# One bank for the first feed-forward product, two pairs of banks in turn for the scores, and new orders for all engines

## The reference, cut to what matters

```
A  x = x + relu(x @ Wd_b.T + bd) @ Wu_b.T + bu         # Wd_b, Wu_b: weights of this batch
   x = layernorm(x) * w + bias, + row of the batch
   h = layernorm(x) * g1 + b1 ;  q, k, v = h @ W_qkv.T
B  s = q @ k.T / 4  (16 heads of 16) ;  p = softmax(s) ;  o = p @ v
C  x = x + (o @ W_o.T) * a1
   h = layernorm(x) * g2 + b2
   x = x + (gelu_tanh(h @ W_f1.T) @ W_f2.T) * a2        # 256 -> 1024 -> 256
D  h = rmsnorm(x) * scale ;  u = h @ up_w.T             # 256 -> 2048
   h = gelu(u[gate]) * u[value] ;  h = quantised to int8 steps per row
   out = x + h @ ternary(down_w).T                      # 1024 -> 256
```

## Time and profile before

| | |
|---|---|
| median of 3 runs | 933.14 us (932.55 to 935.09) |
| the profiled execution's own time | 935.74 us |
| its span, first to last instruction | 933.9 us |
| PE busy | 843.1 us (90%) |
| DVE, ACT, POOL busy | 565.4, 510.9, 231.2 us |
| granted TensorE clock, mean | 0.946 |

### The profile page before, as it was taken

One profiled execution on the slowest core, in us unless ns is written; L12 is line 12 of the kernel. 1 busy time (PEld: TensorE's weight loads), 2 busy tenths in 40 slices (PEclk: granted clock), 3 DMA queues, 4 the chain that ended last, 5 costly groups with the idle time before them and its releaser, 6 DMA issues.

```text
span 933.9 us, 15916 instructions
## 1 busy us (share of the span) xinstructions
PE 843.1 (90%) x5852; PEld 633.5 (68%) x5852; DVE 565.4 (61%) x1063; ACT 510.9 (55%) x796; POOL 231.2 (25%) x333
## 2 busy tenths in 40 slices
...
GB/s 344 365 366 252 248 138 124 148 80 122 62 203 38 135 97 114 120 78 156 47 187 47 188 47 188 46 173 61 154 76 142 65 127 80 104 80 25 24 12 12
DMA packets 58477, 118.48 MB, mean 127 GB/s; under 512 B 6336, under 2 KB 15936, under 8 KB 55696
## 3 DMA queue, kind: packets, MB, share of 16 engines
...
...
## 4 chain that ended last, share of the span: by engine, by line
PE 74%; issue 9%; DMA 7%; DVE 4%; ACT 2%; SPq 2%; POOL 2%; POOLq 0%; DVEq 0%; ACTq 0%
PE bank L486 30%; PE bank L692 11%; PE pair_s L653 6%; PE pair_s L618 5%; PE pair_t L639 5%; PE pair_t L486 4%; DMA hyp<-in_hyper 3%; PE bank L737 3%; PE bank L664 3%; PE bank L567 2%; PE bank L729 1%; PE bank L561 1%; DVE oq L1145 1%; DMA wc<-in_cols 1%; PE bank L574 1%
## 5 line engine op out<-in xcount | busy, mean ns | idle before, releaser
L851 ACT ACTIVATE Pr<-pair_t 128x1024 f32<-128x1024 f32 x128 | 131.3, 1026 | 125.2 <-PE pair_t L639 121.5
L1121 DVE TENSOR_REDUCE nmax<-pair_s 128x4 f32<-128x1024 f32 x128 | 155.8, 1217 | 34.5 <-PE pair_s L618 33.9
L692 PE MATMUL bank<-wf,G 128*128 128x256 f32 x512 | 123.0, 387 | 0.1
L486 PE MATMUL bank<-wup_hi,hD_hi 128*128 128x512 f32 x256 | 109.4, 427 | 4.8 <-POOL hD_lo L1316 4.1
L1344 POOL TENSOR_TENSOR x<-x,xcr 128x512 f32<-128x512 f32 x16 | 20.5, 1281 | 358.1 <-DVE x L1179 358.1
L692 PEld LDWEIGHTS bank<-wf,G 128*128 128x128 f32 x512 | 93.3, 190 | 15.5 <-issue 0.2
L486 PE MATMUL bank<-wup_lo,hD_hi 128*128 128x512 f32 x256 | 102.0, 398 | 0.0
L486 PE MATMUL bank<-wup_hi,hD_lo 128*128 128x512 f32 x256 | 101.9, 398 | 0.0
L618 PE MATMUL pair_s<-Kp,Qp 64*128 64x256 f32 x512 | 66.1, 337 | 21.7 <-DVE nmax L1121 13.0
L895 ACT ACTIVATE gl<-bank,rsD 128x512 f32<-128x512 f32 x64 | 44.1, 689 | 63.6 <-PE bank L486 63.4
L1189 DVE SCALAR_TENSOR_TENSOR hd<-bank,rsD,gl 128x512 f32<-128x512 f32 x64 | 47.9, 748 | 46.2 <-PE bank L486 34.7
...
## 6 DMA issues: line engine op xcount, KB each, us to landing
...
Qp<-qk_scratch SPq DMA_DIRECT2D x64, 256.0 KB, 3.7
Kp<-qk_scratch SPq DMA_DIRECT2D x64, 256.0 KB, 3.6
...
cur_scratch<-gen SPq DMA_DIRECT2D x16, 256.0 KB, 10.1
xT_t<-in_xT SPq DMA_DIRECT2D x16, 256.0 KB, 4.2
```

What stands on the lines that cost most here:

```text
L486: mm = pe.matmul(dst, l, r, start=first and i == 0, stop=last and i == 2)
L692: mm = pe.matmul(bank[5][:, r * D:(r + 1) * D], G[:, k, r * P:(r + 1) * P], wf2[:, k, :], start=k == 0, stop=k == FT - 1)
L851: act.activation(Pr[:, p % 4, :, :].rearrange("p a n -> p (a n)"), pair_t[:, :, :].rearrange("p a n -> p (a n)"), ACT.Exp, scale=DH ** -0. ...
L1121: dve.tensor_reduce(nmax[:, n % 2, :, p % GP, :], pair_s[:, :, :].rearrange("p a (r n) -> p a r n", r=RT), AX.X, ALU.max, negate=True).the ...
```

## The change

- `B.s` slice `p` writes `pair[p % 2]`, and so does `B.t` slice `p`. A slice waits for the reader of the slice two before it. `s0` and `s1` wait for the exponentials of `t6` and `t7` of the batch before, `t0` for the maximum of `s6`, and `t1` for the copy of `m1`.
- `B.m1` moves to bank 2 (`m0` stays in bank 0); `B.o` moves to bank 5.
- All four `C.f` are in bank 5, so `f1` to `f3` each wait for both GELUs of the one before. `C.g0` waits for `tr0`, `B.o0` for the last GELU, `B.o2` for `gate2`, DVE's read of the second feed-forward result.
- `A.k` moves to bank 4 and waits until DVE has read `A.q`; `A.v` waits until DVE has read `A.k`.
- SP waits for all loads of the last turn's heads before it stores new queries or keys.
- The orders of all engines are new, those of head and tail too.

```diff
 FULL = {
     "SP": """
-        C.tc A.load B.m0 B.m1 A.qs A.ks A.ql0 A.ql1 A.kl0 A.ql2 A.kl1 A.kl2 D.y0 A.ql3 D.y1 A.kl3""",
+        C.tc B.m0 A.load B.m1 A.qs A.ql0 A.ql1 A.ks A.ql2 D.y0 A.ql3 A.kl0 A.kl1 A.kl2 A.kl3 D.y1""",
     "PE": """
-        B.s0 A.down C.proj B.s1 A.up D.u0 B.s2 D.u1 C.ht B.s3 D.u2 C.f0 B.m0 C.f1 C.f2 B.s4 A.ht C.f3 B.s5 D.u3 B.t0 B.s6 A.q D.qt0 B.s7 B.t1 A.k D.y0
-        B.t2 B.m1 B.o0 B.t3 C.g0 B.t4 B.o1 A.v B.t5 D.qt1 C.g1 C.g2 B.t6 C.g3 B.t7 D.y1 B.o2 B.o3 C.xt""",
+        B.s0 C.proj D.u0 B.s1 A.down B.s2 B.s3 A.up C.ht D.u1 B.m0 C.f0 D.u2 B.s4 B.s5 C.f1 A.ht D.u3 C.f2 B.s6 B.s7 A.q D.qt0 C.f3 B.m1 B.t0 B.t1
+        D.y0 A.k B.t2 B.t3 B.o0 B.t4 B.o1 B.t5 B.t6 D.qt1 C.g0 C.g1 C.g2 C.g3 B.t7 D.y1 B.o2 B.o3 C.xt A.v""",
     "ACT": """
-        A.down D.u0 C.lnb D.u1 C.ht D.u2 C.f0 A.lnb C.f1 C.f2 A.ht C.f3 D.u3 B.t0 D.qt0 A.q B.t1 A.k B.t2 B.t3 B.t4 B.t5 B.t6 D.qt1 B.t7 A.v C.xt""",
+        D.u0 A.down C.lnb C.ht D.u1 D.u2 C.f0 A.lnb C.f1 A.ht D.u3 C.f2 A.q D.qt0 C.f3 B.t0 B.t1 B.t2 B.t3 B.t4 A.k D.qt1 B.t5 B.t6 B.t7 C.xt A.v""",
     "DVE": """
-        B.s0 C.proj B.s1 C.ln A.up D.u0 B.s2 A.lna D.u1 A.lng B.s3 A.ln B.p0 B.m0 D.quant0 B.s4 D.u2 A.cur B.s5 D.u3 B.s6 B.s7 B.p1 A.q B.m1 A.k
-        D.quant1 D.y0 B.o1 C.g3 D.y1 B.o3""",
+        B.s0 C.proj C.ln B.s1 D.u0 B.s2 B.s3 B.p0 A.up A.lna B.m0 D.u1 A.lng A.ln D.quant0 D.u2 B.s4 B.s5 D.u3 B.s6 B.s7 B.p1 B.m1 A.q D.quant1 A.cur
+        B.o1 A.k D.y0 C.g3 D.y1 B.o3""",
     "POOL": """
-        A.down C.proj C.ln A.up C.ht A.lna A.ln A.ht C.g3 C.xt""",
+        A.down C.proj C.ln C.ht A.up A.lna A.ln A.ht C.g3 C.xt""",
 }
...
 HEAD, turn 0:
-    SP   A.load A.qs A.ks A.ql0 A.kl0 A.ql1 A.ql2 A.ql3 A.kl1 A.kl2 W.late A.kl3
+    SP   W.late A.qs A.load A.ks A.ql0 A.kl0 A.ql1 A.ql2 A.kl1 A.ql3 A.kl2 A.kl3
-    ACT  W.qkv A.down A.lnb A.ht A.q W.fa A.k A.v
+    ACT  A.down W.qkv A.lnb A.ht W.fa A.q A.k A.v
 TAIL, turn 17, PE:
-    C.proj D.u0 D.u1 C.ht D.u2 C.f0 C.f1 C.f2 C.f3 D.u3 C.g0 D.qt0 C.g1 D.y0 C.g2 C.g3 D.qt1 D.y1 C.xt
+    C.proj D.u0 D.u1 C.ht D.u2 C.f0 D.u3 C.f1 D.qt0 C.f2 D.y0 C.f3 D.qt1 C.g0 C.g1 C.g2 C.g3 D.y1 C.xt
...
+        pair = [pair_s, pair_t]
-        F_BANK = [bank[5], bank[2], bank[3], bank[5]]
...
                 def a_k():
-                    if with_c:
-                        pe.wait_ge(act_c, at(ACT_C, "gelu7", c))
-                    else:
-                        past(pe, dve_a, DVE_A, "klo1", a, 1)
+                    pe.wait_ge(dve_a, at(DVE_A, "qlo1", a))
...
                 def a_v():
-                    pe.wait_ge(dve_a, at(DVE_A, "qlo1", a))
+                    pe.wait_ge(dve_a, at(DVE_A, "klo1", a))
...
                 def b_s(p):
-                    if p == 0:
-                        past(pe, dve_m, DVE_M, f"t{NG - 1}", b, 1)
-                        past(pe, dve_o, DVE_O, "tr1", b, 1)
-                    elif p % GP == 0:
-                        pe.wait_ge(dve_m, at(DVE_M, f"t{p // GP - 1}", b))
+                    if p < 2:
+                        past(pe, act_t, ACT_T, f"exp{NP - 2 + p}", b, 1)
                     else:
-                        pe.wait_ge(dve_s, at(DVE_S, f"max{p - 1}", b))
+                        pe.wait_ge(dve_s, at(DVE_S, f"max{p - 2}", b))
+                    if p == GP:
+                        pe.wait_ge(dve_m, at(DVE_M, "t0", b))
...
                 def b_t(p):
-                    if p:
-                        pe.wait_ge(act_t, at(ACT_T, f"exp{p - 1}", b))
-                    elif with_c:
-                        pe.wait_ge(act_c, at(ACT_C, "gelu5", c))
+                    if p >= 2:
+                        pe.wait_ge(act_t, at(ACT_T, f"exp{p - 2}", b))
+                    elif p == 1:
+                        pe.wait_ge(dve_m, at(DVE_M, "t1", b))
                     else:
-                        past(pe, act_t, ACT_T, f"exp{NP - 1}", b, 1)
+                        pe.wait_ge(dve_s, at(DVE_S, f"max{NP - 2}", b))
...
                 def b_o(g):
                     if g == 0:
                         pe.wait_ge(act_a, at(ACT_A, "v", b))
-                        pe.wait_ge(dve_s, at(DVE_S, f"max{NP - 1}", b))
+                        if with_c:
+                            pe.wait_ge(act_c, at(ACT_C, "gelu7", c))
                     if g == 2:
                         pe.wait_ge(dve_o, at(DVE_O, "tr0", b))
+                        if with_c:
+                            pe.wait_ge(dve_c, at(DVE_C, "gate2", c))
...
                 def c_f(n):
                     if n == 0:
                         pe.wait_ge(pool_c, at(POOL_C, "lo", c))
-                    if n == 3:
-                        pe.wait_ge(act_c, at(ACT_C, "gelu1", c))
+                    else:
+                        pe.wait_ge(act_c, at(ACT_C, f"gelu{2 * n - 1}", c))
...
                 def c_g(n):
-                        if not isinstance(a, int) or a < NB:
-                            pe.wait_ge(dve_a, at(DVE_A, "klo1", a))
+                        if b < NB:
+                            pe.wait_ge(dve_o, at(DVE_O, "tr0", b))
...
 SP, at ("A", "qs") and at ("A", "ks"):
+                        if a >= 1:
+                            for j in range(4):
+                                sp.wait_ge(heads_in[j], 32 * a)
```

More of the change, by code:

```diff
@@ L72 @@
     "SP": """
[L73 to L76, removed]
+        0: W.late A.qs A.load A.ks A.ql0 A.kl0 A.ql1 A.ql2 A.kl1 A.ql3 A.kl2 A.kl3 1: B.m0 A.load A.qs B.m1 A.ql0 A.ks A.ql1 A.ql2 A.kl0 2: C.tc 1:
@@ L79 @@
[L79 to L82, removed]
```

103 lines of the change are left out of this document (54 added, 49 removed).

## The result

| | before | after |
|---|---|---|
| median of 4 runs of each on one chip | 934.12 us | 951.79 us (950.68 to 954.84) |
| the profiled execution, and its span | 935.74, 933.9 us | 954.84, 953.0 us |
| granted TensorE clock, mean | 0.946 | 0.935 |

The ratio is 1.0191, with a 95% interval of 1.0176 to 1.0206: 1.9% slower. The prediction said slower, at 938 us, with a range of 914 to 950. The direction was right and the size wrong, by 14 us. The profile of after is the slowest of its four executions, so the profiles differ by 19.1 us of span and the medians by 17.7.

The account below looks back on a forecast made before the run. PE, busy 90% of the span, was taken as the bound. Nine `FULL` turns +3.6 us, tail +3.2 and head -2 sum to +4.8, on the median 933.14 giving 938 us; range 914 to 950.

Parts of the forecast that it names:

- Edges, -2.0 us a turn: `FULL` turn on PE: nine fewer edges between score slices and full-array matmuls, 0.19 us each (1.7), plus 0.3 at `s0`.
- Waits, +2.4 us a turn: `FULL` turn on PE: added waits before `f1` 1.0, `f0` 0.5, around `t3` 0.6, and small ones at `o1`, `s3`, `C.ht`.
- wait 1: `FULL` turn: `C.f1` waits for both GELUs of `f0`, behind `D.u2` and a table load on ACT: 1.0 us.
- Tail, +3.2 us: Turns 14 to 17: +1.2, +0.7, +0.4 and +0.9 us, from fewer edges saved, added waits and turn 17's shared bank.
- Head, -2 us: First turns: removed waits set against later work of turn 2; -2 us taken, from -14 to +6.
- all 13.0 us of waits for maxima: Head: PE's waits of score slices for the previous slice's maximum, ten places, all 13.0 us expected to go.
- 1.48 us of the weights' high part: Head: the weights' high part ahead of `dn`, 1.48 us expected to go.
- projection and feed-forward of turn 2 come some 5 us later: Head: `o3` of turn 1 now stands behind `s0` of turn 2, which waits for its keys: some 5 us.
- Covered by `qt0`, `f3`, `m1`, `t0`, `t1`, `y0` (about 4 us; uncovered it would be some 2 us): `A.q` and `A.k` in one bank: `k`'s wait for DVE's reading of `q` hidden by other PE work.
- rival C: Keys come late, so `s0` of each turn waits: 956 us at two more us a turn, 947 at one; chance 0.12.

Follow-up runs that it names:

- unjoin: Changed kernel with `D.qt1` placed between `t5` and `t6` on PE in `FULL` turns, one slice pair less and two edges more: 956.5 us, a turn of 49.53 us.
- tail_full: Changed kernel with turns 14 and 15 written out in `FULL`'s order on every engine, banks untouched: 950.2 us, ratio 1.0145 to the kernel before.
- tail17: Changed kernel with turn 17's four feed-forward products in banks 5, 2, 3, 5, in the old order except `qt1` ahead of `g3`: 951.5 us, ratio 1.0160.
- head_m1: Changed kernel with turn 1's `B.m1` and `B.t1` ahead of `A.q`, `A.k` behind `t3`, DVE's order to match: 952.6 us, ratio 1.0195.
- fix_bank: head_fix plus head_bank, that is, the reordered head with turn 0's `A.k` in bank 5: 939.0 us, ratio 1.0046 to the kernel before.
- head_fix: Changed kernel with turns 0 and 1 reordered, stage A's chain first, and the up weights' low part moved to turn 2; banks kept: 946.5 us, ratio 1.0126.
- best2: best plus head_bank, and turns 14 and 15 in `FULL`'s order with `C.f0`'s GELUs ahead of `D.u2`: 926.3 us, ratio 0.9898 to the kernel before.
- best: head_fix plus tail17, with ACT taking `C.f0`'s GELUs ahead of `D.u2` in `FULL` and turns 14 to 16: 935.6 us, ratio 0.9996 to the kernel before.
- head_bank: Changed kernel with turn 0's `A.k` in bank 5, waiting for nothing, and `A.v` waiting only for `A.q`'s reading: 955.3 us, ratio 1.0210.
- spload_bank: spload and head_bank together on the changed kernel: 949.6 us, ratio 1.0173 to the kernel before.
- spload: Changed kernel with only SyncE's turn 0 list altered: load of turn 1's sequence first, late weights at the end: 952.1 us, ratio 1.0196.
- head_o3: Changed kernel with `B.o3` of turn 1 ahead of `B.s0` of turn 2 on PE and DVE: 952.4 us, ratio 1.0173.
- head_early: Changed kernel with SyncE's load first in turn 0 and turn 1's `A.down`, `A.up` ahead of its score slices, DVE's order to match: 950.6 us, ratio 1.0149.
- chain1: head_m1 and head_o3 together, with the up weights' low part (4.4 us on DVE) moved from turn 1 to turn 2: 951.9 us, ratio 1.0178.

## Why the prediction was wrong

**Edges, -2.0 us a turn: right.** unjoin measured 0.18 us an edge against 0.19, so nine are 1.6. The measured turn less what its waits cost by starts is 49.18 - 2.2 = 47.0 us, where the prediction had 47.1. The edges at the values' products were taken at 0.19 without a row, and no run isolates them; nor does a row say whether `m1` next to `o0`, both 128*32, is an edge, so the count is nine or eight.

**Waits, +2.4 us a turn: right in kind and place, 2.2.** By starts 0.94 for `f1` (predicted 1.0), 0.5 for `f0` (0.5), 0.53 and 0.20 at `t3` and `t1` (0.6 together), and none in the waits list for `o1`, `s3` and `C.ht` (0.4 together). The Trainium skill (ScalarE: Activation LUTs, What ACT_TABLE_LOAD costs) adds a drain to the load; the estimate from it was 2.4 us for wait 1. The trace does not agree: it was 0.94. The turn came out 0.06 us longer (49.18 against 49.12) instead of 0.4, the nine turns +0.6 us instead of +3.6: two right terms of opposite sign, and a third of a microsecond between them.

**Tail, +3.2 us: +6.3 by `C.proj`, +5.1 by the same work.** Turns 14 to 16 lost 3.5 us by the same work (predicted 2.3), turn 17 lost 1.1 (0.9), and the last 0.4 us are turn 18, which the change doesn't touch. By `C.proj` the turns are +1.1, +2.3 and +1.3, but turn 15's share holds its `A.down`, which before stood ahead of the first of its two marks. The loss of turns 14 and 15 lies in their own orders, as tail_full shows; for turn 15 I counted edges and took the waits as those of `FULL`. Turn 17's goes with the shared bank and the order that came with it (tail17).

**Head, -2 us: +12.0 by `C.proj` of turn 5, +12.9 by the same work. This is the step that failed.** The prediction set "Below: all 13.0 us of waits for maxima" and 1.48 us of the weights' high part against "projection and feed-forward of turn 2 come some 5 us later" and took -2. The 1.48 us came: `A.q` of turn 0 starts 18.2 us after `A.down` and not 19.6. Three things were wrong.

1. The removed waits were not on the chain. Of the 13.0 us, 1.4 lay in turn 16 and not in the head. In turn 1, where most of them were, PE's waits for maxima and for the copies of them (`parts`, `mt`) fell only from 8.3 to 6.7 us, since DVE is busy without a gap from the second maximum of turn 1 to the copy of `m0`; from `s0` to `m0` it is 9.2 us against 8.7 before. PE then waited for `Kp`, `parts`, `q_lo` and `k_lo` instead. head_m1 shows the same once more: a product 7.3 us earlier moved the next turn by 1.2.
2. The shared bank was priced for `FULL` alone. "Covered by `qt0`, `f3`, `m1`, `t0`, `t1`, `y0` (about 4 us; uncovered it would be some 2 us)" holds there: the turn shows no wait for `q_lo`. In turns 0 and 1 stages C and D don't exist, nothing covers it, and the 2 us was paid three times, at 1.84 each. With the order mended it costs 5.4 us of the head (fix_bank against head_fix; 9.3 between best2 and best, whose heads are the same as these two), more than the two gaps of turn 0, 3.7 us. In the first pair 3.1 us are idle time and 2.3 slower matmuls. Without the order it costs nothing that head_bank could show, because SyncE's load holds the keys' store back; with that load out of the way the same edit lets `s0` start 2.3 us earlier (spload_bank against spload).
3. The new order of turn 1 was costed by one move, `o3`, which is worth 1 us or less. What counts is stage A's chain, here behind the score slices: orders alone give 7.3 (best) to 9.2 (head_fix) of the 12.0 us back, and 6 us by the medians. No single piece of that order did: head_m1, head_o3, head_early, spload and chain1 all leave turn 5 at 224.7 to 225.8. That each frees one link while the next, keys of turn 0, `A.down` of turn 1, its queries, its keys, still holds, is my reading of the orders; how the gain divides among them stays open.

The clock added to it: over turns 0 to 4, PE was busy 176.1 us for the work that took 173.2 before, at a granted clock of 0.83 against 0.87. So 2.9 of the 12.9 us are busy time and 10.0 are idle time. Whether the lower clock is cause or consequence of the gaps isn't separated by these runs.

The measured 951.8 us lies between the 947 and 956 of rival C, by luck: no `FULL` turn waits for `Kp`, and the loss is in the head and the tail.
